# Flamingo block: probabilities split ahead of their turn, one turn of squares, ACT lays the squares out

## The reference, cut to what matters

```python
q, k, v = layernorm(x) @ Wq, ctx @ Wk, ctx @ Wv            # 32 heads of 128
score = einsum("bqhd,bkhd->bhqk", q, k) / sqrt(128) + position_bias
probs = softmax(where(mask, score, -inf))                  # zero where masked
x = x + tanh(g_xattn) * (einsum("bhqk,bkhd->bqhd", probs, v) @ Wo)
x = x + tanh(g_ffn) * (layernorm(x) @ W.T + bias + lora(layernorm(x)))
```

## Time and profile before

| | |
|---|---|
| median of 3 runs | 1790.84 us (1790.4 to 1793.89) |
| profiled execution, its time | 1791.13 us |
| its span in the trace | 1789.5 us |
| granted TensorE clock, mean | 0.987 of full speed |
| busy: PE, DVE, ACT, POOL | 97%, 69%, 35%, 34% |
| HBM | 263.54 MB read, 71.30 MB written, 187 GB/s |

### The profile page before, as it was taken

How to read it: one execution, slowest core, us unless ns; L and a number is a source line. 1 busy time by engine, 2 the same in 40 slices (tenths; PEclk the granted TensorE clock), 3 DMA queues, 4 the chain that set the end, 5 groups by cost and what they waited for, 6 DMA issues and landing times.

```text
span 1789.5 us, 25056 instructions
## 1 busy us (share of the span) xinstructions
PE 1734.0 (97%) x8656; PEld 1470.3 (82%) x8656; DVE 1230.5 (69%) x2648; ACT 618.3 (35%) x1224; POOL 615.1 (34%) x812
## 2 busy tenths in 40 slices
PE   5899999999999999999999999999999999999977
PEld 4688888878888888888888888888888888888866
DVE  4677777877776775677767776577767777666663
ACT  3454444444333332233323333233332333223320
POOL 3565656564323322233223322233232322122220
PEclk9899999999999999999999999999999999999988
DMA  4877676866554544545454554455554554445420
GB/s 144 301 251 274 241 277 240 290 248 225 193 188 170 201 154 159 189 166 201 158 187 167 192 178 153 165 191 184 179 173 175 191 174 159 154 159 191 162 95 24
DMA packets 111456, 336.50 MB, mean 188 GB/s; under 512 B 13361, under 2 KB 13489, under 8 KB 111330
## 3 DMA queue, kind: packets, MB, share of 16 engines
q1 hardware_dynamic: 109890, 333.30, 53.1%
q10 hardware_dynamic: 1440, 1.59, 0.3%
HBM read 263.54 MB, written 71.30 MB: 187 GB/s over the span
## 4 chain that ended last, share of the span: by engine, by line
PE 93%; DVE 3%; issue 2%; POOL 1%; ACT 1%; ACTq 0%; DMA 0%; SPq 0%; DVEq 0%
PE vo_bank L275 14%; PE vo_bank L276 14%; PE vo_bank L277 14%; PE q_bank L275 7%; PE q_bank L277 6%; PE q_bank L276 6%; PE k_bank L275 6%; PE k_bank L276 6%; PE k_bank L277 6%; PE pv_two L280 5%; PE s_two L280 5%; PE pv_two L281 2%; PE s_two L281 2%; PE vo_bank L527 1%; DVE score L830 0%
## 5 line engine op out<-in xcount | busy, mean ns | idle before, releaser
L1062 POOL TENSOR_TENSOR score<-score,row_max 128x256 f32<-128x256 f32 x128 | 78.6, 614 | 833.2 <-DVE row_max L835 833.2
L997 POOL TENSOR_TENSOR ot_lo<-attn,ot_hi 128x512 fp32r<-128x512 f32 x128 | 165.3, 1291 | 149.0 <-ACT ot_hi L591 149.0
L275 PE MATMUL vo_bank<-wv,ct_hi 128*128 128x512 f32 x512 | 200.5, 392 | 14.7 <-POOL wv L997 14.7
L275 PE MATMUL q_bank<-xt_hi,wq 128*128 128x512 f32 x512 | 210.2, 411 | 1.4 <-DVE xt_lo L762 1.4
L275 PE MATMUL vo_bank<-wo,ot_hi 128*128 128x512 f32 x512 | 200.4, 391 | 3.7 <-POOL ot_lo L997 3.5
L277 PE MATMUL q_bank<-xt_hi,wq 128*128 128x512 f32 x512 | 202.4, 395 | 0.0
L276 PE MATMUL q_bank<-xt_lo,wq 128*128 128x512 f32 x512 | 201.5, 394 | 0.0
L276 PE MATMUL vo_bank<-wv,ct_hi 128*128 128x512 f32 x512 | 200.2, 391 | 0.0
L277 PE MATMUL vo_bank<-wv,ct_lo 128*128 128x512 f32 x512 | 200.1, 391 | 0.0
L277 PE MATMUL vo_bank<-wo,ot_lo 128*128 128x512 f32 x512 | 200.0, 391 | 0.0
L276 PE MATMUL vo_bank<-wo,ot_hi 128*128 128x512 f32 x512 | 199.9, 390 | 0.0
(11 more groups left out here) (109 smaller groups left out, 3722.5 us busy)
## 6 DMA issues: line engine op xcount, KB each, us to landing
wv<-wv_split SPq DMA_DIRECT2D x96, 512.0 KB, 5.3
wq<-wq_split SPq DMA_DIRECT2D x96, 512.0 KB, 3.3
wk<-wk_split SPq DMA_DIRECT2D x96, 512.0 KB, 3.8
wo<-wo_split SPq DMA_DIRECT2D x96, 512.0 KB, 5.2
raw_bias<-in_pair_bias SPq DMA_DIRECT2D x64, 256.0 KB, 5.7
wq_split<-wq SPq DMA_DIRECT2D x32, 512.0 KB, 2.9
wk_split<-wk SPq DMA_DIRECT2D x32, 512.0 KB, 4.1
wv_split<-wv SPq DMA_DIRECT2D x32, 512.0 KB, 5.8
```

Source lines behind the costliest of these rows:

```text
L275: pe.matmul(to, left[0], right[0], start=first, stop=False)
L997: pool.tensor_tensor(to, src, f32(of), ALU.subtract).then_inc(done, 1)
L1062: pool.tensor_tensor(score[:, :, :], score[:, :, :], row_max[:, :].unsqueeze(2).to_broadcast([P, PB, S]), ALU.subtract).then_inc(shift_don ...
```

## The change

The probabilities are split before they are turned. ACT rounds `prob` into `ph[:, 0]` (128x256), POOL subtracts it into `ph[:, 1]`, one DVE transpose of 128x512 turns the 32x32 squares of both parts into one PSUM bank, and eight ACT copies of 32x256 elements lay the squares out in `pt`, both parts in each. The five DVE transposes, two ACT copies and two DVE subtractions of before are gone. PE waits for `moved` in place of `pt_lo`. ACT's new rounding stands before its `keys(n)`; its eight copies stand where `probabilities(n-1)` stood. POOL's new subtraction stands behind `add_bias(n)`, ahead of its weight parts.

```diff
+        ph = sb("ph", [P, 2, PB, S], F32R)
-        turned = pv_two[:, 0, :, :].rearrange("p a (c s) -> p (a c) s", s=S)
+        turned = pv_two[:, 0:2, :, :].rearrange("p t a (c s) -> p t (a c) s", s=S)
...
             def attention(n):                                   # TensorE
-                pe.wait_ge(pt_lo, n + 1)
+                pe.wait_ge(moved, n + 1)
...
             def probabilities(n):                               # ScalarE
+                act.wait_ge(prob_done, n + 1)
+                wait(act, turn_done, n)
+                hi(ph[:, 0, :, :], prob[:, :, :], ph_hi)
+
+            def squares(n):
+
                 if n == 0:
                     act.wait_ge(pt_zero, PB)
                 wait(act, pv_ps, n)
                 act.wait_ge(turn_done, n + 1)
-                for r in range(2):
-                    rows = cols(r, S)
-                    last = act.activation(pt[rows, :, 0, rows], turned[rows, :, :], ACT.Copy)
-                last.then_inc(pt_hi, 1)
+                for a in range(2):
+                    for i in range(2):
+                        for j in range(2):
+                            to, of = cols(2 * a + i, S // 2), cols(2 * a + j, S // 2)
+                            last = act.activation(pt[to, :, :, of].rearrange("p b t s -> p t b s"),
+                                                  turned[of, :, :, cols(i, S // 2)], ACT.Copy)
+                last.then_inc(moved, 1)
...
             def exps(n):
-                wait(act, turn_done, n)
+                wait(act, ph_lo, n)
...
                 if n > 0:
+                    probabilities(n - 1)
                     keys(n)
                 if n + 1 < H:
                     weights_k(n + 1)
                 if n > 0:
-                    probabilities(n - 1)
+                    squares(n - 1)
...
             def transposes(n):                                  # VectorE
-                dve.wait_ge(prob_done, n + 1)
-                dve.transpose(turned[:, :, :], prob[:, :, :]).then_inc(square_done, 1)
-                dve.wait_ge(square_done, n + 1)
-                for a in range(2):
-                    for i in range(2):
-                        of, to = cols(2 * a + i, S // 2), cols(2 * a + 1 - i, S // 2)
-                        last = dve.transpose(turned[to, :, cols(i, S // 2)], prob[of, :, cols(1 - i, S // 2)])
-                last.then_inc(turn_done, 1)
-
-            def rest_of_probabilities(n):
-                ...
+                dve.wait_ge(ph_lo, n + 1)
+                dve.transpose(turned[:, :, :, :].rearrange("p t b s -> p (t b s)"),
+                              f32(ph[:, :, :, :]).rearrange("p t b s -> p (t b s)")).then_inc(turn_done, 1)
...
             def rest_of_probabilities(n):                       # GpSimd, now called in its slot
+                pool.wait_ge(ph_hi, n + 1)
+                lo(ph[:, 1, :, :], prob[:, :, :], ph[:, 0, :, :], ph_lo)
...
                 add_bias(n)
+                if n > 0:
+                    rest_of_probabilities(n - 1)
                 if n + 1 < H:
                     weights_q(n + 1)
```

More of the change, by code:

```diff
@@ L228, in flamingo_block @@
         q_ps, k_ps, s_ps, pv_ps, vo_ps = (sem(f"{m}_ps") for m in ("q", "k", "s", "pv", "vo"))
[L229 to L232, removed]
+        q_hi, k_hi, vo_hi, ph_hi, ot_hi, wq_hi, wk_hi, wv_hi, wo_hi, stage_hi, lead_ct_hi, lora_hi = (
+            sem(f"{m}_hi") for m in ("q", "k", "vo", "ph", "ot", "wq", "wk", "wv", "wo", "stage", "lead_ct", "lora"))
+        q_lo, k_lo, ph_lo, ot_lo, wq_lo, wk_lo, wv_lo, wo_lo, stage_lo, lead_ct_lo, lora_lo = (
+            sem(f"{m}_lo") for m in ("q", "k", "ph", "ot", "wq", "wk", "wv", "wo", "stage", "lead_ct", "lora"))
         wq_saved, wk_saved, wv_saved, wo_saved, wq_back, wk_back, wv_back, wo_back = (
@@ L241, in flamingo_block @@
             sem(f"{m}_done") for m in ("stats", "aggr", "rstd", "xn"))
-        ident_done, zero_done, seg_done, mask_done, kept_done, half_done, row_done, pt_zero, square_done, turn_done = (
-            sem(f"{m}_done") for m in ("ident", "zero", "seg", "mask", "kept", "half", "row", "pt_zero", "square", "turn"))
+        ident_done, zero_done, seg_done, mask_done, kept_done, half_done, row_done, pt_zero, moved, turn_done = (
+            sem(f"{m}_done") for m in ("ident", "zero", "seg", "mask", "kept", "half", "row", "pt_zero", "moved", "turn"))
         def parts(pair, *at):
@@ L751, in _ @@
             probabilities(LAST)
+            squares(LAST)
             attention_half(LAST)
@@ L924, in slot @@
                     keys(n)
-                    rest_of_probabilities(n - 1)
                     weights_o(n, 1)
@@ L975, in _ @@
             transposes(LAST)
-            rest_of_probabilities(LAST)
             attention(LAST)
@@ L1109, in _ @@
                 slot(n)
+            rest_of_probabilities(LAST)
             attention(LAST)
```

## The result

The changed kernel takes 1853.64 us, the median of 4 runs (1852.83 to 1854.39), against 1790.62 for the kernel before: a ratio of 1.0348, 95% interval 1.033 to 1.0366. It is 63 us slower where 39 were forecast, and 1.6 us above the range.

What follows compares the result with a forecast made beforehand. PE, busy for 97% of the span, was taken to bound the kernel; five terms, 15.6 + 10.8 + 6.7 + 3.9 + 2.5 = 39.5 us of loss, gave 1830 us as a median, range 1804 to 1852.

Steps and rivals of the forecast that it cites:

- relief for DVE: PE's four layernorm turn waits for DVE: taking work off DVE is worth at most those 4.6 us.
- The path: From `prob_done` (probabilities ready) to finished `pt`: 5.34 us after the change instead of 3.62.
- Term A: LoRA and dense jobs in value slots 15, 16, 19, 20 of blocks 1 to 3: 1.3 us lost each, 15.6 us.
- ordinary output slots: Slots making output, not values: `pt` ready at T + 10.86, before attention at T + 11.84, so no loss; still 12.76 us.
- B: Value slots with a piece, blocks 1 to 3: eight groups lose 1.0 us, two lose 1.4; 10.8 us.
- C: Block 0, where POOL's multiplication delays `prob_done` by 0.5 us: value pairs without and with pieces lose 6.7 us together.
- pairs without a piece: Value-slot pairs without a piece in blocks 1 to 3: they come out at T + 11.84, losing nothing, with nothing to spare.
- the clock: PE's granted clock: assumed that stops of 1 to 2 us do not lower it; no loss was priced.
- D: Slots 1 and 2, with no main job to hide in: PE waits for keys and copies, 3.9 us lost.
- Overlap of copies: Rival: ACT's eight copies overlap, path 4.76 us, loss only 14.5 us, about 1806 us; chance 0.20.
- A 32-partition copy: Rival, not slower: it costs half a 64-partition one, eight take 1.5 us, about 1791 us; chance 0.10.
- POOL's subtraction: Rival: it is slow at 1.1 us, path 5.74 us, +33 us, about 1865 us; chance of above 1850 0.08.

Runs made afterwards that it cites:

- e5: The changed kernel with DVE making four of the eight copies only in value slots and in the first two and last two; 1794.09 us, ratio 1.0017.
- e1: The changed kernel with the first value copy ahead of ACT's eight copies in slots where LoRA or dense follows; 1836.5 us, ratio 1.0259.
- e2: The changed kernel with output jobs waiting for the last head's low part (`ot_lo`) only before that head's matmuls; 1846.9 us, ratio 1.0316.
- e3: The kernel before with seven idle 32x256 copies added on ACT behind its `pt` copies, into a scratch tile nobody reads; 1859.16 us, ratio 1.0389.
- e4: The changed kernel with four of ACT's eight copies moved to DVE, behind its keys, in all slots; 1815.4 us, ratio 1.0141.

## Why the prediction was right and wrong

**Right.** That relief for DVE could bring at most a few us; e5 brought 3.5 of the 4.6. The path: 5.34 us forecast, 5.33 measured, with copies at 375 ns and no overlap (eight from first to last in 3.08), the transpose at 0.727 for 0.73, the split at 0.738 for 0.70. Term A's cause, shown by e1 (15.6 forecast, 17.9 by slot lengths, 17.1 by undoing it). That ordinary output slots lose nothing: still 12.76 us.

**Wrong: the step that priced the slots behind a value pair (B, C).** It said "The slot behind it has a turn: ... PE's turn begins at 11.9 where 11.1 was due: 0.8", and for pairs without a piece "nothing, but nothing to spare". It followed the delayed scores only to `prob_done`, and from there to turn and attention. POOL's `ot_lo`, in the same list and just as late, is what PE asks for first, at T + 5.5. Pairs with pieces lost 1.0 by my sum and 1.8 to 2.1 by the trace, but for the two where the sums stand ahead: 1.4 by my sum and 1.0 measured, since the stop at the output job leaves less for the turn; pairs without a piece lost 0.5 to 1.6 each and not zero. B, the pairs without a piece and C came to 36.4 us for 17.5 forecast, 19 of the 23 us that were missing (about 4 of them are the restarts and 1.6 the clock, both below). That this gate takes the delay is shown by e2 (it moves on when the gate opens) and e3 (it takes all of it when the attention takes none).

**Wrong in size: what a stop costs.** I counted from start to start of matmuls, without a restart. PE's waits grew by 46 us and its busy time by 16.6 (1750.6 less 1734.0); slot 51 is 1.42 us longer for 1.12 us idle. Of these 0.30 us, 0.16 are in how idle time is counted: matmuls of 0.39 us start 0.23 apart, and idle begins when the last one ends. My sum, from start to start, had that part. It did not have the other 0.14, the restart: the second matmul after the stop follows after 0.33 us where 0.23 is usual. At twelve stops that is 1.7 of the 2.3 us missing in A. A stop before the attention, whose matmuls are shorter, cost only about 0.02 more than from start to start (slot 40 is 0.36 longer for 0.18 idle).

**Wrong once: the clock.** The prediction assumed that stops of 1 to 2 us do not lower PE's granted clock. Most did not, but behind the one of 1.46 us in slot 28 it fell for 3.4 us and cost 1.6. In D the clock was low for longer than before, and slot 3's 1.20 us, most of the 1.5 that D lacked, is that.

**The rivals.** Overlap of copies did not happen. (The lower bound for it was also mis-worked: 0.11 of overlap off 0.385 gives 8 x 0.27 = 2.2 us, not 2.4.) A 32-partition copy costs what a 64-partition one does, 375 ns against 378. POOL's subtraction was not slow; the time that this rival forecast is near the one measured, but its cause was absent.

The Trainium skill (ScalarE: Activation LUTs, "What ACT_TABLE_LOAD costs") states 186 ns + 0.833 ns a column for an ACTIVATE with immediates, which gives an estimate of 399 ns, and an overlap of about 93 ns between back-to-back ones. The trace has 375 ns and no overlap between these copies, so the measurement decides; with overlap the prediction's own sum had the loss at 14.5 us.

## What to carry to other kernels

When a step delays a chain, list everything that comes out of that chain and when the bounding engine asks for each: the loss falls at the gate that is asked first, and opening it moves the rest to the next. An engine at 35% can still hold the bound up, if a long item stands in its list ahead of the copy that frees a buffer; put such items where nobody waits behind them, and let two engines share them only where both have room (e4 and e5). Before you move work forward in a list, look at when its input is ready as well as at when its output is needed.

## What the runs showed of the hardware that was not expected

- A stop of PE in front of 128x512 matmuls cost 0.14 us beyond the delay of the first one: the first took 0.50 us for 0.39, the second followed after 0.33 us for 0.23. In the list of waits such a stop shows 0.3 us less than it costs.
- ScalarE's copies of 32 and of 64 partitions by 256 columns out of PSUM ran back to back without overlap (375 and 378 ns), while two of 128x512 took 1.08 to 1.09 us for 0.60 each. Out of SBUF, seven of 32x256 took 2.62 us for 0.414 each (e3), an overlap of about 0.05.
- In slot 127 PE's scores came after 2.64 us of idle in the changed kernel and after 2.53 before. The first matmul took 0.55 us and 0.35:

```profile
1789.74 0.55 PE L281 MATMUL s_two<-kt,qt_hi 128*128 128x256 f32 x1 [2.64 <-issue]
...
1729.98 0.35 PE L280 MATMUL s_two<-kt,qt_hi 128*128 128x256 f32 x1 [2.53 <-issue]
```

The first line is of the kernel after, the second of the kernel before. The first is the length at the lower of the two clock levels, as at the start. The clock fell in both: at 1789.7 in the kernel after, at the very start of its scores, and at 1730.5 in the kernel before, 0.5 us into them, where the matmuls of the same size grow to 0.52 us too. The difference is one of a few tenths of a microsecond.
- Stops within the slots can lower the clock too, and not always. Behind one of 1.46 us (slot 28 of the kernel after) it fell for 3.4 us; behind one of 1.44 us in slot 80 it did not. In e3, whose stops in the output slots are the longest, it fell five times, behind stops of 1.89 to 2.86 us, and did not behind others of 1.95 and 1.97 us (slots 41 and 105). What decides it was not tested.
